# A decoder layer on one core: who makes the low parts of the weights in the preparation, how x and the contexts are loaded, and where the query is split in the loop

## The reference, cut to what matters

```python
x = layernorm(x + self_attention(x))           # 16 heads of 16, rotary positions, softmax
x = layernorm(x + cross_attention(x, ctx))     # q = layernorm(x) * gamma + beta, then w_q; 16 heads of 64
x = layernorm(x + moe(x))                      # 8 experts, top 2 of 8, plus a shared expert
# inside cross_attention:
k, v = split(ctx @ w_kv)                       # both 1024 wide
out = (softmax(q * scale @ k.T) @ v) @ w_out + b_out, times tanh(gate)
```

## Time and profile before

| what | value |
|---|---|
| time, median of 3 runs | 715.18 us (712.4 to 716.09) |
| time of the profiled execution | 714.09 us |
| span of the profiled execution, first to last instruction | 712.3 us |
| TensorE busy, matmul | 584.6 us (82%) |
| VectorE busy | 476.7 us (67%) |
| ScalarE busy | 408.8 us (57%) |
| GpSimd busy | 266.8 us (37%) |

### The profile page before, as it was taken

The page is one execution under the profiler, slowest core; times in us unless marked ns, Lnnn a source line. Parts: engine busy times, 40 slices in busy tenths (PEclk is TensorE's granted clock), DMA queues, the critical chain, the costliest instruction groups (busy, mean ns, idle before and its releaser), DMA issues. The chain is left out here.

```text
span 712.3 us, 14305 instructions
## 1 busy us (share of the span) xinstructions
PE 584.6 (82%) x4746; PEld 450.6 (63%) x4746; DVE 476.7 (67%) x903; ACT 408.8 (57%) x995; POOL 266.8 (37%) x295
## 2 busy tenths in 40 slices
PE   4833767899999999989989989989859778899980
PEld 3622656777777777777768768767646454566650
DVE  3795447867877877876876867866766686633332
ACT  2354347577677667567567667664536556643431
POOL 3372014343344344344354245243323721333332
PEclk9975589999999999999999999999975999999995
DMA  8625110210210210210210200220317576333324
GB/s 219 230 104 163 32 62 29 62 43 30 53 50 18 61 50 8 69 43 12 71 38 18 72 28 29 70 91 31 112 38 272 172 260 211 55 61 56 58 30 110
DMA packets 58069, 57.34 MB, mean 81 GB/s; under 512 B 17266, under 2 KB 47218, under 8 KB 58034
## 3 DMA queue, kind: packets, MB, share of 16 engines
q1 hardware_dynamic: 53650, 50.89, 23.2%
q0 software_dynamic: 4384, 5.99, 5.0%
HBM read 46.74 MB, written 10.13 MB: 80 GB/s over the span
## 5 line engine op out<-in xcount | busy, mean ns | idle before, releaser
L656 POOL TENSOR_TENSOR c_rcp<-c_sum,neg_one 112x2 f32<-112x2 f32 x64 | 44.7, 698 | 199.5 <-ACT probs L799 199.5
L660 POOL TENSOR_TENSOR probs<-probs,c_rcp 112x750 f32<-112x750 f32 x64 | 92.0, 1437 | 5.0
L799 ACT ACTIVATE probs<-ps_s,c_neg 112x375 f32<-112x375 f32 x128 | 72.8, 581 | 22.4 <-DVE c_neg L1036 21.9
L691 ACT ACTIVATE kt_hi<-ps_o 128x376 fp32r<-128x376 f32 x64 | 31.9, 498 | 69.1 <-PE ps_o L151 69.1
L1709 POOL DMA_INDIRECT moe_sum<-gsh_hi,xs_in x21 | 33.5, 1594 | 85.9 <-ACT gsh_hi L1757 70.4
L1031 DVE SCALAR_TENSOR_TENSOR v_lo<-ps_vx,v_scale,v_hi 125x512 f16<-125x512 f32 x48 | 35.9, 749 | 41.3 <-ACT v_hi L791 40.8
L1040 DVE SCALAR_TENSOR_TENSOR cpt_lo<-ps_t,cpt_hi 125x672 f16<-125x672 f32 x64 | 54.3, 848 | 12.0 <-ACT cpt_hi L806 12.0
L1036 DVE TENSOR_REDUCE c_neg<-ps_s 112x2 f32<-112x750 f32 x64 | 59.3, 927 | 1.4 <-PE ps_s L151 1.4
L1986 PE MATMUL ps_h<-w_ex,xst_hi 128*128 (+1 forms) x168 | 57.9, 386 | 2.8 <-DVE xst_lo L1796 2.7
L149 PE MATMUL ps_o<-ctxt_hi,w_k_lo 128*128 128x376 f32 x128 | 49.2, 385 | 8.8 <-DVE oct_lo L924 7.7
L1401 PE MATMUL ps_t<-ident,probs 112*128 112x112 f32 x384 | 47.7, 260 | 7.0 <-DVE cpt_lo L1040 6.8
(11 more groups left out here) (315 smaller groups left out, 1794.5 us busy)
## 6 DMA issues: line engine op xcount, KB each, us to landing
chunk<-in_L_ffn_ew_dram SPq DMA_DIRECT2D x24, 512.0 KB, 3.5
spare<-in_L_ffn_ew_dram SPq DMA_DIRECT2D x18, 512.0 KB, 5.7
store<-in_L_ffn_ew_dram SPq DMA_DIRECT2D x6, 512.0 KB, 5.2
ctx_all<-in_ctx_dram SPq DMA_DIRECT2D x2, 1500.0 KB
ctx_raw<-in_ctx_dram SPq DMA_DIRECT2D x8, 375.0 KB
moe_in<-chunk SPq DMA_DIRECT2D x1, 2709.0 KB, 13.9
plain_raw<-in_L_xattn_w_kv_dram SPq DMA_DIRECT2D x2, 1024.0 KB, 15.8
xs_in<-moe_in SPq DMA_DIRECT2D x15, 129.0 KB, 2.0
```

The costliest lines, as they stand in the source:

```text
L656: pool.tensor_tensor(c_rcp[:, s % 2, :], c_sum[:, s % 2, :], neg_one[:, :], ALU.pow).then_inc(sg["c_rcp_ready"], 1)
L660: pool.tensor_tensor(p, p, r, ALU.mult).then_inc(sg["p_normed"], 1)
L799: act.activation(probs[:, s % 2, h, 0:SK], ps_s[0:N, h, 0:SK], ACT.Exp, bias=c_neg[:, s % 2, h:h + 1], accum_out=c_sum[:, s % 2, h:h + 1]) ...
```

## The change

In the preparation all eight halves of the plain weights' low parts are on VectorE: those of weights 0, 1 and 2 behind the rotations of the rounds b0 = 1, 2 and 3, those of weight 3 behind the last round as before. GpSimd keeps the sine products only. The largest magnitude of the value weights moves from ahead of the rounds to behind the rotations of round 0. SyncE loads all of x before the first plain weight, and the contexts as 120 partitions of 25 consecutive rows each, the first 15 and then the other 10; ScalarE sums their magnitudes in five groups of 5 rows (1280 columns), three of them ahead of the second value sum. In the attention, ScalarE and VectorE run place 2 of round 7 (the split of the query) ahead of the split of V01; TensorE's order stays.

```diff
--- before.py
+++ after.py
@@ -64,6 +64,11 @@
 CHUNKS = 3 * (EXP + 1)
 LATE = CHUNKS - 3 * (B - 1)
 P_SCALE = 2.0 ** 14
+CP = 120
+CROWS = B * SK // CP
+CG = 5
+CGR = CROWS // CG
+CG0 = 3
 
 
 
@@ -192,8 +197,8 @@
 
         plain = [(w_o, A["w_out"]), (w_k, A["w_kv"][:, 0:INNER]), (w_v, A["w_kv"][:, INNER:2 * INNER]), (w_q, A["w_q"])]
         plain_raw = [sb(f"plain_raw{i}", [P, 2048]) for i in range(4)]
-        ctx_all = sb("ctx_all", [SKT, B * ST, D])
-        ctx_sum = sb("ctx_sum", [SKT, B])
+        ctx_all = sb("ctx_all", [CP, CROWS, D])
+        ctx_sum = sb("ctx_sum", [CP, CG])
         v_abs = raw[0:N, 0:4, :]
         v_sum = sb("v_sum", [N, 2])
         heads, hw = 2 * H, HD // 2
@@ -219,22 +224,16 @@
                     .then_inc(sg[f"plain{i}"], 16)
 
             load_x(0, slice(0, 2))
-            load_plain(2)
             load_x(1, slice(2, B))
-            for i in (0, 1, 3):
+            for i in (2, 0, 1, 3):
                 load_plain(i)
             sp.dma_start(raw[:, 6:8, :], A["proj_w"].rearrange("(o p) d -> p o d", p=P)).then_inc(sg["raw1"], 16)
-            for h in range(2):
-                sp.dma_start(ctx_all[:, 12 * h:12 * h + 12, :],
-                             A["ctx"][4 * h:4 * h + 4].rearrange("b (t p) d -> p (b t) d", p=SKT)).then_inc(sg[f"ctx_all{h}"], 16)
+            rows = A["ctx"].rearrange("b s d -> (b s) d").rearrange("(p r) d -> p r d", p=CP)
+            for h, r in enumerate((slice(0, CGR * CG0), slice(CGR * CG0, CROWS))):
+                sp.dma_start(ctx_all[:, r, :], rows[:, r, :]).then_inc(sg[f"ctx_all{h}"], 16)
 
         @block.gpsimd
         def _(pool):
-            def plain_lo(i, half):
-                dst, src, part = plain_parts(i, half)
-                pool.wait_ge(sg["plain_hi"], i + 1)
-                pool.tensor_tensor(dst, src, part, ALU.subtract).then_inc(sg["plain_lo"], 1)
-
             pool.dma_start(rope_sb[:, :, :], A["rope"]).then_inc(sg["consts"], 16)
             pool.dma_start(bias_qkv[:, :], A["qkv_b"].partition_broadcast(N)).then_inc(sg["consts"], 16)
             pool.memset(ident[:, :], 0.0).then_inc(sg["zeroed"], 1)
@@ -262,10 +261,6 @@
                         sin = rope_sb[:, 1, dst:dst + hw].unsqueeze(1).to_broadcast([N, heads, hw])
                         pool.tensor_tensor(out[:, :, dst:dst + hw], t[:, :, src:src + hw], sin, ALU.mult)\
                             .then_inc(sg["sin_part"], 1)
-                if b0 in (1, 2):
-                    plain_lo(0, b0 - 1)
-            for half in range(2):
-                plain_lo(1, half)
             pool.wait_ge(sg["consts2"], 5 * 16)
 
         @block.scalar
@@ -310,11 +305,16 @@
             for k in range(KD):
                 act.wait_ge(sg["w_full"], 5 + k)
                 hi(w_proj[0][:, k, :], ps_w[:, k, 256:512]).then_inc(sg["w_hi"], 1)
+            def ctx_magnitude(i):
+                act.wait_ge(sg[f"ctx_all{i // CG0}"], 16)
+                group = ctx_all[:, CGR * i:CGR * i + CGR, :].rearrange("p t d -> p (t d)")
+                act.activation(group, group, ACT.Abs, accum_out=ctx_sum[:, i:i + 1]).then_inc(sg["ctx_sum"], 1)
+
+            for i in range(CG0):
+                ctx_magnitude(i)
             v_magnitude(1)
-            for b in range(B):
-                act.wait_ge(sg[f"ctx_all{b // 4}"], 16)
-                entry = ctx_all[:, ST * b:ST * b + ST, :].rearrange("p t d -> p (t d)")
-                act.activation(entry, entry, ACT.Abs, accum_out=ctx_sum[:, b:b + 1]).then_inc(sg["ctx_sum"], 1)
+            for i in range(CG0, CG):
+                ctx_magnitude(i)
             act.wait_ge(sg["consts2"], 5 * 16)
             act.activation(consts["gate"][:, :], consts["gate"][:, :], ACT.Tanh).then_inc(sg["gate_ready"], 1)
 
@@ -358,9 +358,6 @@
 
             xt_lo(0, 0)
             xt_lo(1, 1)
-            dve.wait_ge(sg["plain2"], 16)
-            dve.wait_ge(sg["zeroed"], 2)
-            dve.tensor_reduce(v_cols[:, 1:2], plain_raw[2][:, :], X, ALU.max, apply_absolute_value=True).then_inc(sg["v_cols"], 1)
             dve.wait_ge(sg["consts"], 32)
             for b0 in range(B // 2):
                 for i in range(2):
@@ -368,10 +365,16 @@
                 if b0 < B // 2 - 1:
                     for i in range(2):
                         xt_lo(2 * b0 + 2 + i, i)
-                if b0 >= 2:
-                    plain_lo(2, b0 - 2)
                 for i in range(2):
                     rotate(2 * b0 + i, i)
+                if b0 == 0:
+                    dve.wait_ge(sg["plain2"], 16)
+                    dve.wait_ge(sg["zeroed"], 2)
+                    dve.tensor_reduce(v_cols[:, 1:2], plain_raw[2][:, :], X, ALU.max, apply_absolute_value=True)\
+                        .then_inc(sg["v_cols"], 1)
+                else:
+                    for half in range(2):
+                        plain_lo(b0 - 1, half)
 
                 dve.wait_ge(sg["rotated"], 2 * b0 + 2)
             for half in range(2):
@@ -381,8 +384,8 @@
                 lo(w_proj[1][:, k, :], ps_w[:, k, 256:512], w_proj[0][:, k, :]).then_inc(sg["wt_lo"], 1)
             dve.wait_ge(sg["v_sum"], 2)
             dve.reduce_max(v_cols[0:N, 2:3], v_sum[:, :], X).then_inc(sg["v_cols"], 1)
-            dve.wait_ge(sg["ctx_sum"], B)
-            dve.reduce_max(v_cols[0:SKT, 0:1], ctx_sum[:, :], X).then_inc(sg["v_cols"], 1)
+            dve.wait_ge(sg["ctx_sum"], CG)
+            dve.reduce_max(v_cols[0:CP, 0:1], ctx_sum[:, :], X).then_inc(sg["v_cols"], 1)
             dve.wait_ge(sg["gate_ready"], 1)
             dve.tensor_scalar(consts["b_out"][:, :], consts["b_out"][:, :], consts["gate"][:, 0:1], None, ALU.mult)\
                 .then_inc(sg["bias_out_gated"], 1)
@@ -887,9 +890,12 @@
                         o_hi(b, s - 2)
                         if more:
                             xn_hi(b + 1)
+                    if s == PAIRS - 1:
+                        place(2)
                     if v_here(b, s, more):
                         v_hi_cross(b if s < 6 else b + 1, V_AT[s])
-                    place(2)
+                    if s < PAIRS - 1:
+                        place(2)
                     if more and s == 0:
                         v_hi(b + 1)
                     if s not in (1, 6):
```

## The result

The changed kernel takes 706.22 us (median of 4 executions, 703.9 to 709.33) against 715.03 us (4 executions, 712.4 to 716.09): ratio 0.9886, interval 0.9841 to 0.9931, so 8.8 us faster. The profiled execution of the changed kernel is the slowest of its four: 709.33 us, span 707.5, where the profiled one of the kernel before took 714.09 us, span 712.3. A second set has six executions of the changed kernel and 17 of the kernel before; one of the 17, at 724.16 us, is a slow one and stays out of every figure here. It gives 704.83 against 715.13 us, ratio 0.9847 (0.98 to 0.9893).

A forecast was written before the change was run, and what follows sets the result against it. VectorE, standing still behind GpSimd, was taken to bound the preparation, and TensorE the loop. Preparation 5.5 plus loop 3.3 gave 8.8 us off: 705.3 from the profile, 706.4 from the median, 706.0 forecast, range 702.0 to 711.0.

The forecast's parts named there:

- the case: Main forecast: preparation gains 4.6 to 6.4 us, loop 2 to 5 us, total 703.8 to 708.6 us; chance 0.55.
- VectorE's standstills are GpSimd's halves: Preparation: three long VectorE instructions stand until GpSimd's low-part halves end; moving the halves removes 12.4 us, adds 4.7.
- The sines' waits stay, 3.4 us: Preparation: each round's cosine product on VectorE still stands until both entries' sines on GpSimd are done, 3.4 us together.
- The stretch of VectorE, 29.2 us: Preparation: VectorE from entry 2's bias to its end, 33.5 - 12.4 + 4.7 + 3.4 = 29.2 us.
- x first: Start: early x removes TensorE's wait, the later maximum adds 2.3 us; entry 2's bias at 26.1 (slow) or 24.3 us (fast).
- Contexts at no cost: Preparation: loading contexts as long rows on 120 partitions costs nothing; at most 0.6 us lost if no faster.
- Query ahead of values, 0.47 us at each of seven boundaries: Attention loop: splitting the query before the values starts the scores 0.47 us earlier at each round boundary, 3.3 us in all.
- The rival that the loop gives nothing back: Softmax chain through VectorE sets the first pair's pace, so only the preparation's 5.5 us are gained, 709.6 us; chance 0.18.
- slow long rows: Preparation: contexts in long rows arrive late, ScalarE's sums hold up VectorE; 732 us at half the load rate; chance 0.03.
- x no earlier: Start: transfers of a queue share engines and finish together, so only 5.3 us gained, 709.9 us; chance 0.08.
- the sines as the cause: Preparation: GpSimd's sines, not its halves, cause VectorE's standstills, which stay; 715.4 us; chance 0.06.
- fewer waits than I count: Fast start and most of the loop's boundary wait gone, 6.4 + 6.3 = 12.7 us gained, 702.5 us; chance 0.10.

The follow-up runs named there:

- the loop's part alone: Kernel before the change, with only the split of the query moved ahead of the split of V01 in round 7: 710.57 us against 715.13, ratio 0.9938.

## Why the prediction was right, and where its terms were off

The total was right: 706.0 forecast, 706.22 measured, inside 702.0 to 711.0. The mechanisms forecast are the ones that the traces show. But the preparation's gain, 8.3 us where 5.5 was forecast, lies outside the 4.6 to 6.4 of the case, and VectorE's last instruction is over at 51.60 us where 53.5 to 55.3 was to show it right.

*VectorE's standstills are GpSimd's halves.* Right: they went, as the end times had said, and putting one block back brought 5.8 us of standing back.

*The sines' waits stay, 3.4 us.* Mis-sized. The step assumed that VectorE stands until the last sine of a round is done. The timeline shows it let in before that: 26.50 + 0.94 = 27.44, when the four sines run until 28.02, and GpSimd's four take 0.44 us longer in turn. The stands are 0.26 + 0.41 us in each of the first two rounds and 0.26 + 0.52 + 0.40 in the third, 2.5 us.

*The stretch of VectorE, 29.2 us.* It measured 51.60 - 24.04 = 27.6. Of the 1.6 us too many, 0.9 are the sines. Another 0.5 is the way from entry 2's bias to the first cosine product, 26.50 - 24.04 = 2.46 us for 2.93 before, because TensorE is now ahead and no bias waits; the sum took that stretch over from before as it was. The last 0.2 is the four added halves: two of them take 2.35 us, but the next instruction starts 2.27 us after them (29.82 to 32.09), so the four cost 4.5 us and not 4.7.

*x first.* The mechanism was right, down to transposes at 15.0 us; of the two speeds offered for entry 1 it was the fast one, 24.04 for the 24.3 worked out, and taking the middle, 25.2, gave 1.2 us away. Putting x back cost 3.8 us, where the working had 28.7 - 24.3 = 4.4 between the fast start and an x that is no earlier.

*Contexts at no cost.* Right, but hardly for the reason that the step gives, longer pieces: with 120 partitions their length changed nothing. The number of engines, which the prediction put beside it, is what the runs show, though the rate grew by half (138 to 202 GB/s) and not threefold. Even with five engines the sums end before VectorE, so the 0.6 us of the lower end was not due either.

*Query ahead of values, 0.47 us at each of seven boundaries.* Right: the wait went from 0.95 and 0.89 to 0.48, the entries from 53.9 to 53.45 us, 3.1 us for 3.3. The rival that the loop gives nothing back is out, by the loop's part alone as well. VectorE's later queue cost nothing to be seen. One row was misread: the 6.7 us of the earlier trace rows are not the seven boundaries. They hold entry 0's first wait (1.29 us at 106.67) and leave out the last boundary (0.72 us at 480.18); the seven come to 6.1 us. The 3.3 does not rest on it, only the upper end and the last rival do.

*The sum.* By the trace it is 8.3 + 3.1 = 11.4 us, where 8.8 was forecast; the medians show 8.8 and 10.3, each known to some 3 us, so they are in reach of 11.4 too. Between the two profiled executions only 4.8 us are left, and there the difference is TensorE's clock after the preparation (9.1 us lost, above). The prediction did not treat that at all: it reckoned from one profiled execution, and the same instructions take 95 to 104 us from one execution to the next. In the executions without a profile nothing shows where the rest of the 11.4 went, or whether it is more than their noise. That the forecast hit within 0.3 us is therefore partly luck: its preparation term was 2.8 us too small by the trace, and the four executions happened to come out about as much behind the trace's sum. The rivals with slow long rows, with x no earlier and with the sines as the cause are each contradicted by a row above; of *fewer waits than I count* the fast start came true and the loop's part did not.

## What to carry to other kernels

When an engine shows durations several times the usual for the same shape, line up their ends with the other engine's runs; work moved off GpSimd can then save VectorE more than it adds (here the standing fell from 12.4 to 2.5 us for 4.5 us of work), and one block left behind keeps the stall. TensorE's wait for a load can cost more than its length when its matmuls are slower behind it, so an early small load in front of a big one is worth more than the gap it closes. Before trusting a sum made against one profiled execution, compare the granted clock by stretches in several: here executions of the same kernel differed by almost as much as the gain looked for.

## What the runs showed of the hardware that was not expected

VectorE and GpSimd do not simply wait for each other's whole run. With only sines queued, VectorE's product got in 0.26 to 0.52 us late and GpSimd took 3.22 us for four (3.75 when a half was asked for instead). With halves queued behind the same sines, VectorE's product stood for 5.8 us, past the sines' end and both halves, and the four sines took their 2.77. The Trainium skill (SBUF — State Buffer, section on the two separate sides) states an exclusive lock, held for a whole instruction by whoever starts first; the single stands of 0.3 to 0.5 us beside a sine of 0.7 agree. Who comes next when both wait is another matter: no run here settles why VectorE came next in the one case and not in the other.

A matmul of 256 columns took 0.41 us at some times and 0.28 at others (14.81 and 17.53 us in the changed kernel, shown above) while the granted clock read 1.00 for both, in the stretch table:

```profile
11.00:15.00 4.00, 3.93 (x12) 3.22 (x13) 0.99 (x2) 0.00 (x0) 0.10 (x1) 1.00 0.91 275
15.00:18.00 3.00, 3.00 (x18) 2.42 (x16) 1.27 (x3) 0.36 (x1) 1.39 (x3) 1.00 1.08 387
```

So that column alone does not tell the durations to expect in the first 20 us.
